# Causal linear attention in 64-token halves with eight-tile matmuls

## What is computed

```python
def favor(x, omega):                       # per head: 16 numbers in, 16 features out
    u = einsum("bshd,dm->bshm", xs, omega)
    return concatenate([exp(u - h), exp(-u - h)], -1) * m ** (-0.5)

def step(carry, qkv):                      # over the tokens, causal
    Sst = Sst + ki[..., :, None] * vi[..., None, :]
    zst = zst + ki
    num = einsum('bhm,bhmd->bhd', qi, Sst)
    den = einsum('bhm,bhm->bh', qi, zst) + ATTN_EPS
```

## Time and profile before

| | us |
|---|---|
| median of 3 runs | 2659.86 |
| lowest and highest | 2656.11, 2664.98 |
| the profiled execution, first to last instruction | 2655.4 |
| TensorE busy | 2582.9 |
| VectorE busy | 2113.7 |
| ScalarE busy | 1545.3 |
| GpSimd busy | 1426.2 |

### The profile page before, as it was taken

How to read it: one execution, slowest core, us unless ns; L and a number is a source line. 1 busy time by engine, 2 the same in 40 slices (tenths; PEclk the granted TensorE clock), 3 DMA queues, 4 the chain that set the end, 5 groups by cost and what they waited for, 6 DMA issues and landing times.

```text
span 2655.4 us, 61603 instructions
## 1 busy us (share of the span) xinstructions
PE 2582.9 (97%) x21416; PEld 2135.6 (80%) x21416; DVE 2113.7 (80%) x5242; ACT 1545.3 (58%) x3137; POOL 1426.2 (54%) x1406
## 2 busy tenths in 40 slices
PE   7899999999999999999898999999999999999998
PEld 4688888888888888888776788888888888888886
DVE  5788877786777777888899888887898888888775
ACT  3544455445544454445346776777767777776772
POOL 2244344343343445445476666665666667776664
PEclk9999999999999999999999999999999999999999
DMA  3100000010000010000111000000110110100001
GB/s 90 36 17 10 17 2 17 14 35 2 1 2 7 12 37 18 18 17 25 47 50 52 28 17 10 14 17 14 30 33 22 33 32 23 33 30 25 26 27 45
DMA packets 77731, 65.63 MB, mean 25 GB/s; under 512 B 15394, under 2 KB 72698, under 8 KB 77434
## 3 DMA queue, kind: packets, MB, share of 16 engines
q1 hardware_dynamic: 77434, 61.70, 7.9%
HBM read 49.10 MB, written 12.58 MB: 23 GB/s over the span
## 4 chain that ended last, share of the span: by engine, by line
PE 92%; DVE 3%; issue 2%; ACT 1%; DMA 1%; SPq 0%; POOL 0%; DVEq 0%; ACTq 0%; POOLq 0%
PE PS L273 81%; PE PS L981 4%; PE PS L943 1%; PE PS L1011 1%; PE PS L934 1%; PE PS L486 1%; PE PS L424 1%; PE PS L476 1%; PE PS L892 1%; PE PS L1041 1%; DVE PS L3573 1%; DVE U L3165 0%; ACT PR L2236 0%; DMA QSB<-in_L_ffn_k_scale 0%; DMA ZS<-xs_scratch 0%
## 5 line engine op out<-in xcount | busy, mean ns | idle before, releaser
L2236 ACT ACTIVATE PR<-PS,SM 128x256 f32<-128x256 f32 (+1 forms) x512 | 280.3, 560 | 137.4 <-DVE SM L3578 135.7
L1922 ACT ACTIVATE FB<-PS,BC 128x512 f32<-128x512 f32 x192 | 133.5, 695 | 327.6 <-PE PS L273 188.5
L3165 DVE TENSOR_TENSOR U<-PS,CST 128x512 f32<-128x512 f32 x384 | 238.2, 682 | 40.3 <-PE PS L273 39.9
L4604 POOL TENSOR_TENSOR RL<-FB,RH 128x512 fp32r<-128x512 f32 x96 | 125.9, 1312 | 236.4 <-DVE RH L3143 236.4
L273 PE MATMUL PS<-W2H,RH 128*128 128x256 f32 x768 | 226.0, 294 | 7.4 <-POOL RL L4604 7.4
L4826 POOL TENSOR_TENSOR SM<-SM,COL 128x8 f32<-128x8 f32 x128 | 224.7, 1756 | 10.6
L3573 DVE CUSTOM_DVE_ANT_0 PS<-PS,MSK 128x256 f32<-128x256 f32 (+1 forms) x512 | 202.5, 436 | 31.1 <-PE PS L273 30.2
L273 PE MATMUL PS<-W2H,RL 128*128 128x256 f32 x768 | 215.8, 281 | 0.0
L273 PE MATMUL PS<-W2L,RH 128*128 128x256 f32 x768 | 215.6, 281 | 0.0
L4616 POOL TENSOR_TENSOR SBD<-SBD,TMP 128x256 f32<-128x256 f32 x84 | 64.5, 768 | 213.6 <-DVE TMP L3157 213.6
L273 PEld LDWEIGHTS PS<-W2H,RH 128*128 128x128 f32 x768 | 145.1, 189 | 30.2 <-issue 25.6
(11 more groups left out here) (264 smaller groups left out, 8745.3 us busy)
## 6 DMA issues: line engine op xcount, KB each, us to landing
PX<-in_L_attn_x SPq DMA_DIRECT2D x16, 512.0 KB, 4.1
TB<-in_k_rot SPq DMA_DIRECT2D x64, 128.0 KB, 2.1
SG<-in_L_attn_W SPq DMA_DIRECT2D x24, 256.0 KB, 2.7
xp_scratch<-PX SPq DMA_DIRECT2D x8, 512.0 KB, 2.9
xs_scratch<-X SPq DMA_DIRECT2D x64, 64.0 KB, 1.5
ZS<-xs_scratch SPq DMA_DIRECT2D x16, 256.0 KB, 2.9
GG<-xp_scratch SPq DMA_DIRECT2D x7, 512.0 KB, 3.8
out<-GG SPq DMA_DIRECT2D x7, 512.0 KB, 3.0
```

Of the source, the lines that this page charges most:

```text
L1922: e.activation(FB[:, hb % 2, :], PS[:, 5, :], ACT.Relu, bias=BC[:, l % 2, 4 + hb:5 + hb]).then_inc(*a_re.up(n, hb))
L2236: t = e.activation(PR[:, par, 256 * i + lo:256 * i + hi], PS[:, 3 + par, 256 * i + lo:256 * i + hi], ACT.Exp, bias=S[:, 40 + 2 * g + i:41 ...
L3165: e.tensor_tensor(heads(U[:, u % 6, :], 4), heads(PS[:, g, :], 4), bcast(CM, 4), ALU.mult).then_inc(*d_mk.up(n, u))
L4604: e.tensor_tensor(RL[:, r, :], FB[:, 0, :], RH[:, r, :].bitcast(F), ALU.subtract).then_inc(*p_rl.up(n, hb))
```

## The change

Scores, states and sums are made over tiles of 64 tokens, two of them (h = 0, 1) side by side in the array, and a chunk's new states are made ahead of its scores.

- `scores(n, j)`: 16 matmuls of 32 rows, 64 weight columns and 128 moving columns in place of 8 of 32 rows, 128 and 256. Only the first half of each bank is used.
- `masks(n, j)`: two operations of 512 elements, each over two banks, in place of four; four slots of U in place of six.
- `new_states(n)`, new: after `turn_k`, 64 matmuls of 64 rows, 32 weight columns and 32 moving columns into banks 0 and 1, for all eight half tiles. ScalarE's `keep_states(n)` copies them to U[:, 4]. `scores(n, 0)` waits for that copy.
- GpSimd: `key_states` adds them up (128x64 each) and writes each sum as a block diagonal (128x256, a broadcast multiply with BM) to one of four slots. `key_state`, VectorE's `state` and TMP are gone.
- `sums(n, j)`: for each h, the state product as 8 matmuls of 128 rows, 32 weight columns and 64 moving columns; then 32 masked products of 64 rows, 32 and 64. The result lies in banks 4 and 5 (one per h), 128 columns each. Bank 5 is also that of `up`, so `sums` waits for the relu of the last `up`, and `up` for the last `numerators`.
- The order: `sums(n, 3)` stands before `turn_h`, `up(m, 7)` before `down(m, 4)`, and `up(m, 5)` before `down(m, 2)`.
- The triangle constant repeats for 64 tokens.

```diff
+        def new_states(n):
+            for i in range(2):
+                e.wait_ge(*a_kt.at(n, i))
+                e.wait_ge(*d_v.at(n, i))
+            for j in range(4):
+                for m in range(2):
+                    for c in range(4):
+                        for h in range(2):
+                            r = slice(64 * h, 64 * h + 64)
+                            a = D * (j % 2) + 128 * m + 32 * c
+                            t = mm(e, PS[32 * c:32 * c + 32, h, 64 * j + 32 * m:64 * j + 32 * m + 32], KS[r, j // 2, a:a + 32],
+                                   value_places(VP[r, j, :])[:, 4 * m + c, :, :], j == 0 and m == 0)
+            t.then_inc(*e_ds.up(n))
...
         def scores(n, j):
             if j == 0:
+                e.wait_ge(*a_ds.at(n))
...
-                        e.wait_ge(*d_mk.at(n, 4 * j - 4 + g))
-                    t = mm(e, PS[:, g, 256 * m:256 * m + 256].rearrange("p (o q) -> p o q", o=2), FK[32 * g:32 * g + 32, m, 128 * j:128 * j + 128],
-                           FQ[32 * g:32 * g + 32, m, 1:3, 128 * j:128 * j + 128], m == 0)
+                        e.wait_ge(*d_mk.at(n, j - 1, g // 2))
+                    for h in range(2):
+                        q = 128 * j + 64 * h
+                        t = mm(e, PS[64 * h:64 * h + 64, g, 128 * m:128 * m + 128].rearrange("p (o q) -> p o q", o=2), FK[32 * g:32 * g + 32, m, q:q + 64],
+                               FQ[32 * g:32 * g + 32, m, 1:3, q:q + 64], m == 0)
...
-        def sums(n, j):
+        def sums(n, j, relued=None):
...
+            if relued:
+                e.wait_ge(*a_re.at(*relued))
+            for h in range(2):
+                t = 2 * j + h
+                if t == 0 and n % 4 == 0:
+                    continue
+                e.wait_ge(*(p_sd.at(n, t - 1) if t else p_sd.at(n - 1, 7)))
                 for m in range(2):
-                    mm(e, PS[:, 4, 128 * m:128 * m + 128], SBD[:, tile % 2, m, :], FQ[:, m, 0, 128 * j:128 * j + 128], m == 0)
...
+                    for c in range(4):
+                        mm(e, PS[32 * c:32 * c + 32, 4 + h, 64 * m:64 * m + 64], block_state(t)[:, m, 32 * c:32 * c + 32],
+                           FQ[:, m, 0, 128 * j + 64 * h:128 * j + 64 * h + 64], m == 0)
...
+                        for h in range(2):
+                            r = slice(64 * h, 64 * h + 64)
...
+                            t = mm(e, PS[32 * g:32 * g + 32, 4 + h, 64 * m:64 * m + 64], VP[r, j, v:v + 32], masked(j, g // 2)[r, a:a + 64], alone and m == 0 and odd == 0)
...
-        def up(n, hb):
+        def up(n, hb, read=None):
+            if read:
+                e.wait_ge(*a_nu.at(*read))
...
+            new_states(n)
+            key_sums(n)
             scores(n, 0)
-            key_sums(n)
+            up(m, 5)
             down(m, 2)
-            up(m, 5)
-            sums(n, 0)
+            sums(n, 0, (m, 5))
             scores(n, 1)
-            up(m, 6)
+            up(m, 6, (n, 0))
             down(m, 3)
-            sums(n, 1)
+            sums(n, 1, (m, 6))
             scores(n, 2)
+            up(m, 7, (n, 1))
             down(m, 4)
-            up(m, 7)
-            sums(n, 2)
+            sums(n, 2, (m, 7))
             scores(n, 3)
             down(m, 5)
+            sums(n, 3)
             turn_h(w)
             down(m, 6)
             if n < 23: turn_x(n + 1)
-            if n < 23: up(w, 0)
-            sums(n, 3)
+            if n < 23: up(w, 0, (n, 3))
...
+        def keep_states(n):
+            e.wait_ge(*e_ds.at(n))
+            e.copy(U[:, 4, :].rearrange("p (h x) -> p h x", h=2), PS[:, 0:2, 0:256]).then_inc(*a_ds.up(n))
...
         def masks(n, j):
             e.wait_ge(*e_sc.at(n, j))
-            for g in range(4):
-                u = 4 * j + g
-                if u >= 6:
-                    e.wait_ge(*e_u.at(n, (u - 6) // 4))
-                e.tensor_tensor(heads(U[:, u % 6, :], 4), heads(PS[:, g, :], 4), bcast(CM, 4), ALU.mult).then_inc(*d_mk.up(n, u))
+            if j >= 2:
+                e.wait_ge(*e_u.at(n, j - 2))
+            for i in range(2):
+                o = masked(j, i).rearrange("p (g x q) -> p g x q", g=2, x=4)
+                a = PS[:, 2 * i:2 * i + 2, 0:256].rearrange("p g (x q) -> p g x q", x=4)
+                e.tensor_tensor(o, a, CM[:, 0:64].unsqueeze(1).unsqueeze(1).broadcast_to([128, 2, 4, 64]), ALU.mult).then_inc(*d_mk.up(n, j, i))
...
+        def add_state(n, t):
...
+            last = half_states((t - 1) % 2, (t - 1) // 2) if t else CC[:, :]
+            new = CC[:, :] if t == 7 else half_states(t % 2, t // 2)
+            e.tensor_tensor(new, half_states(t % 2, t // 2), last, ALU.add).then_inc(*p_cs.up(n, t))
+
+        def block_diagonal(n, t):
...
+            e.tensor_tensor(block_state(t + 1).rearrange("p m (r e) -> p m r e", r=4), src,
+                            BM.rearrange("p (r e) -> p r e", r=4).unsqueeze(1).broadcast_to([128, 2, 4, 32]), ALU.mult).then_inc(*p_sd.up(n, t))
...
             low_hidden(m, 2)
+            key_states(n, 0, 1, 2)
             add_bo(n)
-            key_state(n, 0)
             low_hidden(m, 4)
             rsqrt(("1", w))
+            key_states(n, 3, 4)
             low_hidden(m, 6)
-            key_state(n, 1)
-            key_state(n, 2)
+            key_states(n, 5, 6)
```

More of the change, by code:

```diff
@@ L620, in _ @@
         turn_k(0, 1)
+        new_states(0)
+        key_sums(0)
         scores(0, 0)
-        key_sums(0)
         sums(0, 0)
@@ L645, in _ @@
         turn_k(1, 1)
+        new_states(1)
+        key_sums(1)
         scores(1, 0)
-        key_sums(1)
         scores(1, 1)
@@ L678, in _ @@
         up(0, 4)
+        new_states(2)
+        key_sums(2)
         scores(2, 0)
-        key_sums(2)
+        up(0, 5)
         down(0, 2)
         down(0, 3)
-        up(0, 5)
-        sums(2, 0)
+        sums(2, 0, (0, 5))
         scores(2, 1)
-        up(0, 6)
+        up(0, 6, (2, 0))
         down(0, 4)
-        sums(2, 1)
+        sums(2, 1, (0, 6))
         scores(2, 2)
-        up(0, 7)
-        sums(2, 2)
+        up(0, 7, (2, 1))
+        down(0, 5)
+        sums(2, 2, (0, 7))
         scores(2, 3)
-        down(0, 5)
+        down(0, 6)
+        sums(2, 3)
         turn_h(1)
         turn_x(3)
-        sums(2, 3)
         spread(2)
-        up(1, 0)
-        down(0, 6)
+        up(1, 0, (2, 3))
         up(1, 1)
@@ L719, in _ @@
         down(1, 1)
+        new_states(3)
+        key_sums(3)
         scores(3, 0)
-        key_sums(3)
         up(1, 4)
         down(1, 2)
-        sums(3, 0)
+        sums(3, 0, (1, 4))
         scores(3, 1)
+        up(1, 5, (3, 0))
         down(1, 3)
         down(1, 4)
-        up(1, 5)
-        sums(3, 1)
+        sums(3, 1, (1, 5))
         scores(3, 2)
+        up(1, 6, (3, 1))
         down(1, 5)
-        up(1, 6)
-        sums(3, 2)
+        sums(3, 2, (1, 6))
         scores(3, 3)
-        up(1, 7)
+        up(1, 7, (3, 2))
+        down(1, 6)
+        sums(3, 3, (1, 7))
         turn_h(2)
         turn_x(4)
-        down(1, 6)
-        up(2, 0)
-        sums(3, 3)
+        up(2, 0, (3, 3))
         spread(3)
@@ L763, in _ @@
         up(2, 4)
+        new_states(4)
         key_sums(4)
@@ L804, in _ @@
         up(3, 4)
+        new_states(5)
+        key_sums(5)
         scores(5, 0)
-        key_sums(5)
+        up(3, 5)
         down(3, 2)
-        up(3, 5)
-        sums(5, 0)
+        sums(5, 0, (3, 5))
         scores(5, 1)
@@ L1160, in _ @@
         up(21, 4)
+        new_states(23)
+        key_sums(23)
         scores(23, 0)
-        key_sums(23)
         up(21, 5)
         down(21, 2)
-        sums(23, 0)
+        sums(23, 0, (21, 5))
         scores(23, 1)
-        up(21, 6)
-        sums(23, 1)
+        up(21, 6, (23, 0))
+        down(21, 3)
+        sums(23, 1, (21, 6))
         scores(23, 2)
-        down(21, 3)
-        up(21, 7)
-        sums(23, 2)
+        up(21, 7, (23, 1))
+        down(21, 4)
+        sums(23, 2, (21, 7))
         scores(23, 3)
-        down(21, 4)
+        down(21, 5)
+        sums(23, 3)
         turn_h(22)
-        sums(23, 3)
         spread(23)
         turn_tile(0)
-        up(22, 0)
-        down(21, 5)
+        up(22, 0, (23, 3))
         down(21, 6)
@@ L2034, in _ @@
         relu(0, 4)
+        keep_states(2)
         relu(0, 5)
+        numerators(2, 0)
         relu(0, 6)
-        numerators(2, 0)
         numerators(2, 1)
+        relu(0, 7)
         numerators(2, 2)
+        numerators(2, 3)
         high_mid(1, 0)
@@ L2043, in _ @@
         high_row(3, 1)
-        relu(0, 7)
-        numerators(2, 3)
         relu(1, 0)
@@ L2090, in _ @@
         relu(2, 4)
+        keep_states(4)
         relu(2, 5)
@@ L2118, in _ @@
         relu(3, 4)
+        keep_states(5)
         relu(3, 5)
@@ L2320, in _ @@
         relu(20, 4)
+        keep_states(22)
         relu(20, 5)
@@ L2324, in _ @@
         numerators(22, 1)
+        relu(20, 7)
         numerators(22, 2)
-        relu(20, 7)
```

(6 more changed lines are left out.)

278 lines of the change are left out of this document (127 added, 151 removed).

## The result

The changed kernel takes 2763.33 us (median; 2759.26 to 2770.19), the kernel before 2658.12 (2656.11 to 2664.98) beside it: a ratio of 1.0397, with an interval of 1.0383 to 1.0411. The forecast was 2605 with a range of 2566 to 2652, and "slower" had 0.17. It is 105 us slower, and both rivals on that side named another cause than the runs show.

The account below looks back on a forecast made before the run. TensorE's stream was taken as the bound: -4.0 + 0.3 + 1.45 = -2.25 us a chunk, 49.5 over 22 chunks, plus 5 for chunks 0 and 1, gives span 2600.9; with 4.5 more, 2605 us, range 2566 to 2652.

Parts of the forecast that it names:

- both rivals on that side: The two slower cases: row halves taking turns, 2687 us, chance 0.11; a floor under small passes, 2847 us, chance 0.06.
- the price of a round: TensorE's new phases: a round of eight passes of 32 or 64 columns was taken as 0.055 us.
- no charge: Moving sums(n, 3) ahead of turn_h and up(w, 0) costs nothing, since the cover of turn_h's casts stays.
- What bounds the kernel: In chunks 2 to 23 of the first half, time is what TensorE's stream takes; a saved microsecond counts unless a wait returns.
- TensorE's block, 12.86 to 8.9 us: Sums, scores, key_sums and new_states on TensorE together take 4.0 us less a chunk, eight tiles running at once.
- rival (c): TensorE's two row halves take turns, so a round of eight costs two of four: slower, 2687 us; chance 0.11.
- Rival (d): TensorE can start no pass sooner than 27 ns, so the 640 small passes cost 17.3 us: 2847 us; chance 0.06.
- Wait 1: scores(n, 0) waits for ScalarE's copy of the new states out of banks 0 and 1: 0.3 us lost a chunk.
- Wait 2: sums(n, 0) waits for relu(m, 5), which waits for VectorE's masks, normaliser and RL: 1.5 us lost a chunk.
- GpSimd's part of the forecast: Three state pairs of 1.2 us go ahead of add_bo and low_hidden(m, 4); slack 1.0 us, so nothing lost.
- Slack 2 us or more: GpSimd's state pairs 3 to 6, made two by two in 2.4 us, come that early for sums 2 and 3.
- a gain of 1 where 5 were taken: Chunks 0 and 1 together were to gain 5 us from shorter steps, bounds 0 and 12.

Follow-up runs that it names:

- the long blocks at 32 and 64 columns: Program of TensorE matmuls alone, no waits inside, computing nothing of the kernel: 1024 passes over eight tiles took 26.7 us at 32 columns, 27.8 at 64.

## Why the prediction was wrong

Three steps of the sum failed: a pass was counted by its columns and its start and never by the supply of instructions (about 2.0 us a chunk), a wait was counted at its own length without the slow clock behind it (at most 1.9 us), and GpSimd's moved add was held only against GpSimd's own deadline and not against VectorE (1.0 us). Smaller ones are the price of a round (0.9 us) and the "no charge" for sums(n, 3) (0.5 us).

**What bounds the kernel.** Right, and the chunk table bears it out: TensorE's stream is the time, and whatever makes it wait or slows it counts in full.

**TensorE's block, 12.86 to 8.9 us.** The mechanism was right and a term mis-sized. All eight tiles run together, so rival (c) is out: at 128 columns a round of eight takes 0.110 us, what a round of four took. But the round was put at 0.055 us for 32 and for 64 columns. At full clock it is 0.068 at 32 ((1.22 - 0.13) / 16, from undisturbed new_states of 1.22 us from start to next) and 0.082 at 64 ((0.79 - 0.13) / 8, from undisturbed masked phases of 0.79 us). Undisturbed, new_states takes 1.22 us (forecast 1.0), scores 0.62 (0.59), sums 1.37 (1.23); with key_sums 9.75 us instead of 8.9. The gain would still have been 3.1 us a chunk.

**Instruction supply.** Missing. The forecast counted a pass only by its columns and its start. 640 passes for 224 a chunk, in dense blocks, outrun the supply: 33 gaps, 43.8 us, 2.0 us a chunk. Rival (d) had the right number, 27 ns a pass, by luck and in the wrong form: it was taken from a round of four at 128 columns. As a floor under every pass it would have made 187 us; as a limit on how long a dense stream can go on it bites only where several dense phases meet, and the wide matmuls between them let the supply catch up. The Trainium skill ("TensorE: Matmul & The Clock Gate", Back-to-back issue gap) gives about 25 ns a matmul for 64 columns or fewer. The means of the long blocks at 32 and 64 columns, 26 and 27 ns, lie near this figure, but here they come from the packets. Inside a burst the run does not agree: 8.5 to 14 ns a pass over eight tiles up to 128 columns.

**Wait 1, 0.3 us.** Right in kind, and smaller: key_sums with the wait behind it takes 0.75 us in most chunks, 0.18 more than before. The mean of 0.96 in the table contains two gaps of the instruction supply, in chunks 9 and 18.

**Wait 2, 1.5 us.** The chain was right link by link, and the size right for a VectorE that works alone (1.55 us in the run with add_bo first). The step that failed is in GpSimd's part of the forecast. This took add_bo's new place 3.6 us later only as a matter of GpSimd's own deadline, and didn't ask what VectorE would be doing then. That is 1.0 us a chunk.

**The clock after a wait.** Missing. The sum put a wait down at its own length. In the kernel before with the wait alone, 13 stretches of half clock, 3.4 us each, follow the waits of 2.06 us, and cost 1.45 us a chunk on top of them. The relu's wait is not the only one that brings it: with VectorE's low half earlier 41.0 us at half clock are left, and with fewer passes besides 23.3, and in the changed kernel the stretches at 1042.9 and 1206.7 us follow gaps of the supply. For the changed kernel 75.1 us at half clock between 110 and 1270 us (some 20 chunks) bound this cost at 37.6 us, 1.9 us a chunk.

**sums(n, 3), "no charge".** Wrong: 0.46 us a chunk in the loop. In chunks 2 to 5 TensorE waits five times for X0L and X1L, 8.3 us together; that this has the same cause was not tried by itself. The prediction looked at what the moved work waits for and not at whom it had covered.

**GpSimd and the first chunks.** The add of 128x64 is 0.32 us (0.35 taken) and the block diagonal 0.73 to 0.74 where nothing disturbs it; right. "Slack 2 us or more" for the pairs behind it held in the loop, but not in chunks 3 and 5: their sums wait for SBD, 4.4 us together, where the kernel before has one such wait of 1.7 us. From the key_sums of chunk 0 to that of chunk 2 it is 96.8 us against 97.9, a gain of 1 where 5 were taken. The granted clock in 54.2 to 108.4 us is 0.84 against 0.97; what it cost there stays open.

**The account.** From -2.25 to +4.74 a chunk is 7.0 us: block 0.9, supply 2.0, wait 1 -0.1, wait 2 1.0, sums(n, 3) 0.5, half clock at most 1.9. At least 0.8 us stays open; gaps of the supply that are shorter than 0.7 us or lie in other phases are part of it.

## What to carry to other kernels

Splitting matmuls into more and smaller passes is paid in instructions: count them for a dense stretch, and see whether it uses up 256 of them in less than about 3.5 us. When a step is moved, ask three things of it: what it waits for, whom it covered in its old place, and what runs beside it in the new one, above all VectorE with two SBUF operands beside GpSimd. A wait of 2 us on a TensorE that never idled is not 2 us but what it costs together with the slow clock behind it, here 3.6 us.
